# A four-layer graph network on one core: probability pieces at step ends in the score banks, own banks for second queries and keys, and a new order at several places

## The chip, the cores and the metric

The kernel runs on one core of one Trainium2 chip. The metric is the device time of one execution in microseconds (us), as the median of several runs. The engines are TensorE (PE: matmuls and transposes, whose weight loads are listed as PEld), VectorE (DVE), ScalarE (ACT), GpSimd (POOL) and SyncE (SP, which issues the DMAs here). Each has its own queue and works through it in order; they meet at semaphores.

## What is computed

`x` is 16 x 512 x 256, `adj` is a 512 x 512 matrix of zeros and ones. Four layers follow each other, each with a residual sum and a layer norm:

```python
x = _layernorm(x + L0(x, adj, Wq, Wk, Wv))   # rel = (x Wq^T)(x Wk^T)^T * adj^T, rows divided by their norm, times x Wv^T
x = _layernorm(x + L1(x, adj, weight, bias)) # normalized adjacency times x W, plus bias
x = _layernorm(x + L2(x, adj, adj, ...))     # three gated steps, below
x = _layernorm(x + L3(x, adj, ...))          # attention, 8 heads of 32, masked by adj, and an output product
```

One step of layer 2, done three times on h:

```python
a_in = a_out = einsum('nm,bmd->bnd', adj, h); av = concatenate([a_in, a_out])
z = sigmoid(lin(av, w3) + lin(h, u3));  r = sigmoid(lin(av, w4) + lin(h, u3))
hv = tanh(lin(av, w5) + lin(r * h, u5))
h = (1 - z) * h + z * hv
```

## The kernel before, in words

**Passes.** `passes` (L196) runs the body of every engine 18 times. In pass k, batch i = k goes through layers 0 to 2, batch t = k - 1 through the third norm and attention, and batch o = k - 2 through the rest of its attention (pieces 14 and 15, the last values product, the output product) and the fourth norm. Where a role has no batch (at the start and the end) its parts are left out. The order of the work in every queue is written out by hand, one role's instructions between the other's.

**High and low words.** A product with fp32 accuracy is made of three matmuls (`mm3`, L842 to L845): high by high, low by high, high by low. So every operand is split: ACT copies the high words (the lines with `copy(..[H]..)`), DVE subtracts them from the source for the low words (`tile_lo`, L659, and others). TensorE waits for both.

**PSUM** has eight banks, `ps[:, 0]` to `ps[:, 7]`. Banks 0 to 3 serve layers 0 to 2, banks 4 and 5 the two score tiles of a pair, the x3 transposes and the output product, bank 6 (PT_BANK) the transposed probabilities, bank 7 (O_BANK) the values product. The first queries and keys, `qk_of(0)` and `qk_of(1)`, use banks 6 and 7, the second ones, `qk_of(2)` and `qk_of(3)`, banks 0 and 1 (`QK_BANK`, L120).

**Layers 0 to 2 of batch i.** `y_of` (x times a product of weights), `gram` (four tiles, L967, the relation), DVE's mask product `rel_of` (L678), the relation product into u, the square sums (L1036 to L1042: POOL adds squares, sixteen small matmuls sum them, DVE copies them at L730, POOL takes the power -0.5 at L326), the sums and statistics of the first norm (L653, L627, L634, L639; POOL's power at L293), `gather` (L862, the adjacency product) of layer 1, its weight product, the second norm (`normalize`, L644), the transposes of the state (L1084), and then three steps j of layer 2: u3, gather, w4, w5, wd, u5 on TensorE; gate tanh L503 and L514 and value tanh L527 on ACT; the chain L819, L821, L822 on DVE, once for each half d, that makes the new state; the transposes of the state L1167 back to natural order, and its low words L826 and L829.

**Attention of batch t.** It has 32 score tiles in 16 pairs k. `score(k)` (L921) writes the two tiles of a pair to banks 4 and 5; DVE's `masked` (L672) masks them and finds the row maximum; ACT's `exponentials` (L395); POOL's `probabilities` inverts the row sum (L298) and scales (L304); TensorE's `back(k, c)` transposes the pair in two pieces c of four 128 x 128 blocks each (L945) into bank 6; ACT's `prob_copy` (L390) empties the bank; after four pairs a `values` product (L957). Step j of layer 2 has the pairs Z, D_, A, B_, C, E = 4j + 2 to 4j + 7 between its products. Piece (k, c) waits for the copy of the piece before it, since all use bank 6:

```python
            pe.wait_ge(pt_c, b * TILES + (2 * k + c))
```

The end of a step on TensorE, before:

```python
            if t is not None:
                back(t, A, 0)
                values(t, j)
                back(t, A, 1)
                if j == 0:
                    score(E)
            ...
            for d in range(DT):
                ...   # wait for h_f, four transposes of the state half d, L1167
                if t is not None:
                    back(t, B_, d)
```

**Queues beside it.** SP issues four small DMAs for each of the eight head slots (L238). Those of heads 4 to 7 wait for the score tiles of pairs 4 to 7 (L234). POOL splits the input x (L286, L288) right behind the powers of the third norm, and subtracts the low words of the next x^T (L268) late in the pass.

Of the kernel before, what the change touches and what calls it, by code (L numbers as in the profile page):

```python
# [19 lines left out]
def gnn_stack(nc, x, x_t, adj, wq0, wk0, wv0, w1, b1, w3, bw3, u3, bu3, w4, bw4, w5, bw5, u5, bu5,  # L20
# [16 lines left out]
    with ExitStack() as ctx:  # L37
# [82 lines left out]
        QK_BANK = (6, 7, 0, 1)  # L120
# [8 lines left out]
        def half(c):  # L129
            return slice(2 * c, 2 * c + 2)  # L130

# [228 lines left out]
        def _(act):  # L360
# [22 lines left out]
            def body(i, t, o):  # L383
                def prob_copy(b, k, c):
# [5 lines left out]
                    copy(pT[:, k % SLOTS, half(c)], ps[:, PT_BANK, :].rearrange("p (a b) -> p a b", a=2)).then_inc(pt_c, 1)  # L390
# [92 lines left out]
                for j in range(STEPS):  # L483
# [27 lines left out]
                    if i is not None:  # L511
                        for d in range(DT):
                            act.wait_ge(z_ps, m + (d + 1))
                            nc.scalar.activation(tz[:, d], ps[:, 2 + d], ACT.Tanh, bias=cols[:, BZ, d:d + 1],  # L514
                                                 scale=0.5).then_inc(z_t, 1)
                        if j == STEPS - 1:
                            xT_hi(i + 1)
                    if t is not None:
                        if j == 0:
                            exponentials(t, A)  # L520
                        prob_copy(t, D_, 0)
# [9 lines left out]
                    if i is not None and j < STEPS - 1:  # L531
                        h_hi(0)
                    if t is not None:
# [3 lines left out]
                    if i is not None and j < STEPS - 1:  # L537
                        h_hi(1)
                    if t is not None:
                        prob_copy(t, B_, 0)  # L540
# [4 lines left out]
                    if t is not None:  # L545
                        prob_copy(t, B_, 1)
# [4 lines left out]
        def _(dve):  # L551
# [58 lines left out]
            def body(i, t, o):  # L610
# [94 lines left out]
                if i is not None:  # L705
                    rel_of(0)
# [5 lines left out]
                if i is not None:  # L712
                    rel_lo(0)
                    rel_of(1)
# [10 lines left out]
                if t is not None:  # L725
                    qk_lo(0)
                    qk_lo(1)
                if i is not None:
                    dve.wait_ge(ssq_ps, i + 1)
                    nc.vector.tensor_copy(ssq[:, :], ps[:, 0, 0:NT]).then_inc(ssq_c, 1)  # L730
                    dve.wait_ge(rn_r, i + 1)
# [28 lines left out]
                if t is not None:  # L760
                    qk_lo(2)
                    qk_lo(3)
                if i is not None:
                    normalize(xg, xg, 1, 0, i, x2_r)
                    normalize(xg, xg, 1, 1, i, x2_r)
                    for c in range(2):
                        dve.wait_ge(xn_h, i * 6 + (c + 1))
                        TT(XNS[:, L, half(c)], xg[:, half(c)], f32(XNS[:, H, half(c)]), ALU.subtract).then_inc(xn_l, 1)
                if t is not None:
                    masked(1)  # L770
                if i is not None:
# [67 lines left out]
        def _(pe):  # L839
# [22 lines left out]
            def gather(xs, ready, value, signal):  # L862
# [9 lines left out]
                pe.wait_ge(ready, value + 1)  # L872
                node_tile(1, 0, (H,))
# [44 lines left out]
            def body(i, t, o):  # L918
                first = isinstance(i, int) and i == 0

                def score(k):  # L921
# [5 lines left out]
                    for u in range(2):  # L927
                        if k > 0:
                            pe.wait_ge(ttr, t * TILES + (2 * k - 1 + u))
                        q = 2 * (k % 8 // 4) + u  # L930
# [3 lines left out]
                def back(b, k, c):  # L934
                    if c == 0:
                        pe.wait_ge(nrm, b * TILES + (2 * k + 2))
                    if k == 0 and c == 0:
                        pe.wait_ge(vv_r, b + 1)
                    else:
                        pe.wait_ge(pt_c, b * TILES + (2 * k + c))  # L940
                    dst = ps[:, PT_BANK, :].rearrange("p (a b) -> p a b", a=2)
# [7 lines left out]
                def values(b, m):  # L949
                    gr, hf = m // 2, m % 2  # L950
                    pe.wait_ge(pt_c, b * TILES + 8 * (m + 1))
                    if m == 2:
# [14 lines left out]
                def gram(s):  # L967
                    c = slice(s * P, (s + 1) * P)
                    for d in range(DT):
# [17 lines left out]
                if i is not None:  # L987
                    if not first:
                        pe.wait_ge(x3a, i * 2)
                    gram(0)  # L990
                if o is not None:
                    back(o, 15, 0)
                if i is not None:
                    gram(1).then_inc(s_ps, 1)
# [102 lines left out]
                for j in range(STEPS):  # L1097
                    Z, D_, A, B_, C, E = [4 * j + k for k in range(2, 8)]
                    if i is not None:
# [55 lines left out]
                    if t is not None:  # L1155
# [3 lines left out]
                        if j == 0:  # L1159
                            score(E)  # L1160
# [38 lines left out]
```

## Time and profile before

| | us |
|---|---|
| runs | 2326.36, 2326.69, 2326.75 |
| median | 2326.69 |
| the profiled execution, its own time | 2327.76 |
| its span, first to last instruction | 2326.0 |
| TensorE busy in the span | 2099.9 (90%) |
| DVE busy | 1548.3 (67%) |
| ACT busy | 1267.0 (54%) |
| POOL busy | 979.5 (42%) |

The page of the profile gives shares of the span; since the kernel repeats one pass, a stretch of the timeline from one `y_of` to the next is the better thing to read. Pass 8 runs from 1112.4 to 1249.5 us. In a timeline a row is a start, a duration, the engine and line, what is written and read, how often, and, in brackets, how long the engine idled before it and which instruction ended that. Matmuls overlap, so their durations add up to more than their starts show.

### The profile page before, as it was taken

The page shows a single profiled execution, that of the slowest core. Times are in us where ns is not written, and L with a number is a line of the kernel's source. Part 1 is how long each engine was busy: PE and PEld are TensorE (multiplying, and loading weights), DVE is VectorE, ACT ScalarE, POOL GpSimd, SP SyncE. Part 2 cuts the span into 40 slices and gives each one's busy share as a digit, 9 for nine tenths or more (in the row PEclk, how much of TensorE's full clock was granted, in tenths as well). Part 3 has the DMA queues.
Part 4 walks back from the last instruction along what each step waited for, and adds up shares of the span by engine and source line. Part 5 has one row for each costly group of instructions (what it writes and reads, how often), then busy time and mean ns, then how long its engine had stood idle before and what let it go on. Part 6 is the DMA issues. An engine that isn't in the chain of part 4 may idle for free.

```text
span 2326.0 us, 34745 instructions
## 1 busy us (share of the span) xinstructions
PE 2099.9 (90%) x12342; PEld 1655.9 (71%) x12342; DVE 1548.3 (67%) x3423; ACT 1267.0 (54%) x2516; POOL 979.5 (42%) x1138
## 2 busy tenths in 40 slices
PE   5888999999999999999999999999999999999965
PEld 4666777777777777777777777777777777777743
DVE  5556676676667667666776767677676767767642
ACT  3235646566564656646465564646556464655644
POOL 3013534445353444535444453444435344443533
PEclk8899999999999999999999999999999999999987
DMA  3003021120202112021120301112030111202030
GB/s 122 1 19 70 7 52 46 37 64 19 63 20 55 46 37 64 19 53 30 52 50 28 73 19 41 42 39 62 19 73 28 37 46 37 64 19 67 16 90 10
DMA packets 65617, 101.16 MB, mean 43 GB/s; under 512 B 11425, under 2 KB 31137, under 8 KB 65441
## 3 DMA queue, kind: packets, MB, share of 16 engines
q1 hardware_dynamic: 65440, 98.87, 16.7%
q8 instruction: 103, 1.69, 0.3%
q14 instruction: 74, 0.60, 0.1%
HBM read 23.34 MB, written 8.39 MB: 14 GB/s over the span
## 4 chain that ended last, share of the span: by engine, by line
PE 62%; DVE 21%; ACT 9%; issue 6%; POOL 2%; DMA 1%; SPq 0%; DVEq 0%; POOLq 0%; ACTq 0%
PE ps L843 12%; PE ps L845 12%; PE ps L844 12%; PE ps L865 11%; PE ps L945 6%; PE ps L931 4%; DVE fa L821 4%; DVE fa L819 3%; DVE stats L627 3%; ACT pT L390 2%; DVE xn L653 2%; ACT fa L395 2%; DVE xn L644 2%; PE ps L957 2%; DVE fa L822 2%
## 5 line engine op out<-in xcount | busy, mean ns | idle before, releaser
L672 DVE CUSTOM_DVE_ANT_0 fa<-ps,mask 128x512 f32<-128x512 f32 x512 | 332.1, 685 | 284.8 <-PE ps L931 284.5
L298 POOL TENSOR_TENSOR rsum<-esum,mhalf 128x2 f32<-128x2 f32 x256 | 199.1, 778 | 756.4 <-ACT fa L395 756.4
L304 POOL TENSOR_SCALAR fa<-fa,rsum 128x512 f32<-128x512 f32 x512 | 421.7, 837 | 53.0 <-POOL rsum L298 53.0
L945 PE MATMUL ps<-ident,fa 128*128 128x128 f32 x2048 | 325.3, 282 | 97.7 <-ACT pT L390 85.7
L390 ACT COPY pT<-ps 128x512 f32<-128x512 f32 x512 | 298.8, 584 | 172.6 <-PE ps L945 172.6
L945 PEld LDWEIGHTS ps<-ident,fa 128*128 128x128 f32 x2048 | 243.6, 143 | 205.3 <-ACT pT L390 89.9
L395 ACT ACTIVATE fa<-fa,nmax 128x512 f32<-128x512 f32 x512 | 366.0, 724 | 32.2 <-DVE nmax L672 32.2
L659 DVE TENSOR_TENSOR ra<-ps,ra 128x512 fp32r<-128x512 f32 x224 | 151.1, 686 | 244.2 <-ACT ra L493 140.6
L865 PE MATMUL ps<-adjT,ra 128*128 128x512 f32 x1024 | 259.6, 407 | 27.5 <-DVE ra L745 25.3
L865 PEld LDWEIGHTS ps<-adjT,ra 128*128 128x128 f32 x1024 | 195.8, 194 | 79.0 <-issue 33.5
L931 PE MATMUL ps<-ra 128*128 128x512 f32 x512 | 179.8, 433 | 4.8 <-DMA ra<-ra 4.7
L293 POOL TENSOR_TENSOR rstd<-veps,mhalf 128x2 f32<-128x2 f32 x128 | 96.7, 762 | 168.1 <-DVE veps L639 168.1
L843 PE MATMUL ps<-ra,W_u 128*128 128x512 f32 x384 | 158.7, 413 | 0.0
L843 PE MATMUL ps<-ra,W_w 128*128 128x512 f32 x384 | 155.0, 404 | 0.0
L844 PE MATMUL ps<-ra,W_u 128*128 128x512 f32 x384 | 153.2, 399 | 0.0
L845 PE MATMUL ps<-ra,W_u 128*128 128x512 f32 x384 | 153.0, 398 | 0.0
L845 PE MATMUL ps<-ra,W_w 128*128 128x512 f32 x384 | 152.2, 396 | 0.0
L844 PE MATMUL ps<-ra,W_w 128*128 128x512 f32 x384 | 152.0, 396 | 0.0
L514 ACT ACTIVATE fa<-ps,cols 128x512 f32<-128x512 f32 x96 | 66.3, 690 | 114.0 <-PE ps L845 114.0
L957 PE MATMUL ps<-pT,vf 128*32 128x256 f32 x2048 | 127.7, 391 | 0.7 <-ACT pT L390 0.7
L493 ACT CAST ra<-ps 128x512 fp32r<-128x512 f32 x96 | 56.3, 586 | 115.0 <-PE ps L865 115.0
L843 PE MATMUL ps<-ra 128*128 128x512 f32 x256 | 107.6, 420 | 8.1 <-DVE ra L659 6.0
(183 smaller groups left out, 4653.1 us busy)
## 6 DMA issues: line engine op xcount, KB each, us to landing
ra<-ra SPq DMA_DIRECT2D x512, 128.0 KB, 2.4
fa<-in_x_T SPq DMA_DIRECT2D x17, 512.0 KB, 4.7
fa<-in_x SPq DMA_DIRECT2D x17, 512.0 KB, 3.9
out<-fa SPq DMA_DIRECT2D x16, 512.0 KB, 2.9
fa<-in_L_gnn_w_w SPq DMA_DIRECT2D x3, 512.0 KB, 8.3
adj_n<-in_adj SPq DMA_DIRECT2D x1, 1024.0 KB, 5.6
fa<-in_L_gnn_u_w SPq DMA_DIRECT2D x2, 256.0 KB, 9.3
fa<-in_L_gnn_Wk SPq DMA_DIRECT2D x1, 256.0 KB, 5.8
```

The lines of the kernel that those rows point to most:

```text
L298: nc.gpsimd.tensor_tensor(rsum[:, 2 * k:2 * k + 2], esum[:, 2 * k:2 * k + 2], mhalf[:, 4:6], ALU.pow).then_inc(rs_r, 1)
L304: nc.gpsimd.tensor_scalar(SC[:, g], SC[:, g], rsum[:, 2 * k + u:2 * k + u + 1], 1.0, ALU.mult, ALU.mult).then_inc(nrm, 1)
L390: copy(pT[:, k % SLOTS, half(c)], ps[:, PT_BANK, :].rearrange("p (a b) -> p a b", a=2)).then_inc(pt_c, 1)
L395: nc.scalar.activation(SC[:, s % RING], SC[:, s % RING], ACT.Exp, bias=nmax[:, s:s + 1], scale=-1.0, accum_out=esum[:, s:s + 1]).then_inc( ...
L672: nc.vector.tensor_tensor_reduce(out=SC[:, s % RING], in0=ps[:, 4 + u], in1=mask[:, 2 * (k % 8 // 4) + u], scale=-1.0, scalar=3.0e38, op0= ...
L843: mm(dst, w_h, m_h, start=first, stop=False, skip_group_check=again)
L844: mm(dst, w_l, m_h, start=False, stop=False, skip_group_check=again)
L845: return mm(dst, w_h, m_l, start=False, stop=last, skip_group_check=again)
L865: ins = mm(ps[:, q, :], xs[:, p, s, q * P:(q + 1) * P], adjT[:, H, s], start=s == 0 and p == H, stop=s == NT - 1 and p == L)
L931: mm(ps[:, 4 + u, :], STK[:, slot, 0, q * P:(q + 1) * P], STK[:, slot, 1, :], start=True, stop=True).then_inc(sc_ps, 1)
L945: ins = nc.tensor.transpose(dst[:, a, u * P:(u + 1) * P], SC[:, (2 * k + u) % RING, kt * P:(kt + 1) * P], ident[:, :])
L957: ins = mm(ps[e * HD:(e + 1) * HD, O_BANK, hf * 2 * P:(hf + 1) * 2 * P], vf[:, kt, head * HD:(head + 1) * HD], pT[:, (4 * m + e) % SLOTS, kt],
```

## The change

1. `pt_bank(k, c)`: the pieces of pairs 5, 9 and 13 (B_ of each step) go to banks 4 and 5 instead of bank 6. They wait for the masking of the score tiles that are in these banks, not for the copy of the piece before; score pairs 7 and 12 wait for their copies.
2. TensorE at the end of a step: piece (B_, d) comes ahead of the transposes of the state half d, not behind. `score(7)` moves from the end of step 0 to step 1, between u3 and the gather.
3. ACT: in step 0 the copy of piece (D_, 0) and the exponentials of A move between the two tanh of the z gate. At the end of every step the copies of the pieces of A come ahead of the high copy of the first state half, and both pieces of B_ ahead of the high copies of the transposed state.
4. Second queries and keys go to banks 1 and 7 instead of 0 and 1. `qk_of(3)` waits for the copy of the values' input (vv_r), the gather of step 0 waits for the low words of the second queries only behind its first two node tiles, the first values product for all four.
5. DVE: the second norm's `normalize` comes ahead of `qk_lo(2)` and `qk_lo(3)`, of which one moves between the two low-word subtractions of the normed state and one behind `masked(1)`.
6. DVE: the copy of the square sums comes ahead of `qk_lo(1)`.
7. DVE: the third norm's `normalize` comes ahead of the mask product `rel_of(0)`.
8. TensorE: piece (15, 0) of the old batch moves between the two halves of `gram(0)`.

```diff
-        QK_BANK = (6, 7, 0, 1)
+        QK_BANK = (6, 7, 1, 7)
+        def pt_bank(k, c):
+            return 4 + c if k in (5, 9, 13) else PT_BANK
...
-                    if i is not None:
-                        for d in range(DT):
+                    for d in range(DT):
+                        if i is not None:
                             act.wait_ge(z_ps, m + (d + 1))
                             nc.scalar.activation(tz[:, d], ps[:, 2 + d], ACT.Tanh, bias=cols[:, BZ, d:d + 1],
                                                  scale=0.5).then_inc(z_t, 1)
-                        if j == STEPS - 1:
-                            xT_hi(i + 1)
+                        if t is not None and j == 0 and d == 0:
+                            prob_copy(t, D_, 0)
+                            exponentials(t, A)
+                    if i is not None and j == STEPS - 1:
+                        xT_hi(i + 1)
                     if t is not None:
-                        if j == 0:
-                            exponentials(t, A)
-                        prob_copy(t, D_, 0)
+                        if j > 0:
+                            prob_copy(t, D_, 0)
...
                         prob_copy(t, A, 0)
-                    if i is not None and j < STEPS - 1:
-                        h_hi(0)
-                    if t is not None:
                         prob_copy(t, A, 1)
                         if j == STEPS - 1:
                             exponentials(t, E)
                     if i is not None and j < STEPS - 1:
+                        h_hi(0)
+                    if t is not None:
+                        prob_copy(t, B_, 0)
+                    if i is not None and j < STEPS - 1:
                         h_hi(1)
                     if t is not None:
-                        prob_copy(t, B_, 0)
+                        prob_copy(t, B_, 1)
...
-                if i is not None:
-                    rel_of(0)
                 if t is not None:
...
                     normalize(x3, xg, 2, 0, t)
                     normalize(x3, xg, 2, 1, t, x3_r)
                 if i is not None:
+                    rel_of(0)
                     rel_lo(0)
...
                     qk_lo(0)
-                    qk_lo(1)
                 if i is not None:
                     dve.wait_ge(ssq_ps, i + 1)
                     nc.vector.tensor_copy(ssq[:, :], ps[:, 0, 0:NT]).then_inc(ssq_c, 1)
+                if t is not None:
+                    qk_lo(1)
...
-                if t is not None:
-                    qk_lo(2)
-                    qk_lo(3)
                 if i is not None:
                     normalize(xg, xg, 1, 0, i, x2_r)
                     normalize(xg, xg, 1, 1, i, x2_r)
-                    for c in range(2):
+                for c in range(2):
+                    if i is not None:
                         dve.wait_ge(xn_h, i * 6 + (c + 1))
                         TT(XNS[:, L, half(c)], xg[:, half(c)], f32(XNS[:, H, half(c)]), ALU.subtract).then_inc(xn_l, 1)
+                    if t is not None and c == 0:
+                        qk_lo(2)
                 if t is not None:
                     masked(1)
+                    qk_lo(3)
...
                 node_tile(0, 1)
                 pe.wait_ge(ready, value + 1)
+                if second is not None:
+                    pe.wait_ge(second, second_value)
...
+                        if k in (7, 12):
+                            pe.wait_ge(pt_c, t * TILES + (2 * (5 if k == 7 else 9) + u + 1))
...
+                    elif pt_bank(k, c) == PT_BANK:
+                        pe.wait_ge(pt_c, b * TILES + (2 * k + c - (2 if c == 0 and pt_bank(k - 1, 1) != PT_BANK else 0)))
                     else:
-                        pe.wait_ge(pt_c, b * TILES + (2 * k + c))
+                        pe.wait_ge(ttr, b * TILES + (2 * (k + (1 if k == 5 else 2)) + c + 1))
...
+                    if m == 0:
+                        pe.wait_ge(qk_l, b * 4 + 4)
...
-                    gram(0)
+                    gram(0, (0,))
                 if o is not None:
                     back(o, 15, 0)
                 if i is not None:
+                    gram(0, (1,))
                     gram(1).then_inc(s_ps, 1)
...
                     qk_of(2)
+                    pe.wait_ge(vv_r, t + 1)
                     qk_of(3)
...
-                        elif t is not None:
-                            pe.wait_ge(qk_l, t * 4 + 4)
-                        gather(XNS, xn_l, m + 1, a_ps)
+                    if t is not None and j == 1:
+                        score(7)
+                    if i is not None:
+                        gather(XNS, xn_l, m + 1, a_ps, qk_l if j == 0 and t is not None else None, (t or 0) * 4 + 3)
...
-                        if j == 0:
-                            score(E)
...
                     for d in range(DT):
+                        if t is not None:
+                            back(t, B_, d)
                         if i is not None:
                             pe.wait_ge(h_f, m + (d + 1))
...
-                        if t is not None:
-                            back(t, B_, d)
```

## Rows read from the trace of the kernel before

**Rows 1.** The page's first line: span and instructions.
```profile
span 2326.0 us, 34745 instructions
```

**Rows 2.** Windows: stretch, its length, busy us (instructions) by engine, clock, DMA share, GB/s.
```profile
1112.40:1249.50 137.10, 128.21 (x772) 101.75 (x771) 95.66 (x214) 78.28 (x156) 60.95 (x71) 1.00 0.17 43
...
2209.00:2300.00 91.00, 60.87 (x366) 40.68 (x364) 35.35 (x103) 46.52 (x105) 37.73 (x56) 0.79 0.24 58
```

**Rows 3.** Waits of TensorE in pass 8: us in total, times, longest.
```profile
PE ps L945 <- ACT pT L390: 4.3, 7, 1.2
```

**Rows 4.** Timeline of TensorE around the ends of steps 2, 0 and 1.
```profile
1112.05 0.66 PE L945 MATMUL ps<-ident,fa 128*128 128x128 f32 x4
1112.46 0.48 PE L843 MATMUL ps<-ra,W_g 128*128 128x512 f32 x1
...
1182.17 0.40 PE L845 MATMUL ps<-ra,W_u 128*128 128x512 f32 x1
1183.82 0.66 PE L945 MATMUL ps<-ident,fa 128*128 128x128 f32 x4 [1.25 <-ACT pT L390]
...
1191.39 0.66 PE L1167 MATMUL ps<-ident,fa 128*128 128x128 f32 x4 [0.19 <-DVE fa L822]
...
1192.94 0.48 PE L843 MATMUL ps<-ra,W_u 128*128 128x512 f32 x1
...
1219.66 0.66 PE L1167 MATMUL ps<-ident,fa 128*128 128x128 f32 x4 [0.20 <-DVE fa L822]
...
1221.20 0.48 PE L843 MATMUL ps<-ra,W_u 128*128 128x512 f32 x1
```

**Rows 5.** Timeline of TensorE in the first half of pass 8.
```profile
1117.40 0.50 PE L843 MATMUL ps<-ra 128*128 128x512 f32 x1 [0.34 <-DVE ra L659]
...
1123.87 1.09 PE L1004 MATMUL ps<-ident,xn 128*128 128x128 f32 x8 [0.47 <-DVE xn L644]
...
1126.76 0.50 PE L843 MATMUL ps<-ra 128*128 128x512 f32 x1
...
1146.84 3.98 PE L865 MATMUL ps<-adjT,ra 128*128 128x512 f32 x16 [1.08 <-DVE ra L745]
...
1161.67 3.97 PE L865 MATMUL ps<-adjT,ra 128*128 128x512 f32 x16 [0.17 <-DVE ra L768]
```

**Rows 6.** Timeline of DVE in pass 8.
```profile
1120.24 1.23 DVE L678 TENSOR_TENSOR fa<-ps,adj_n 128x1024 f32<-128x1024 f32 x1 [2.40 <-PE ps L845]
1121.38 2.44 DVE L644 TENSOR_SCALAR xn<-xn,mv,rstd 128x256 f32<-128x256 f32 x4
...
1137.89 0.75 DVE L686 SCALAR_TENSOR_TENSOR ra<-ps,cols,ra 128x512 fp32r<-128x512 f32 x1 [2.44 <-ACT ra L419]
1138.55 0.15 DVE L730 COPY ssq<-ps 128x4 f32<-128x4 f32 x1
1139.84 0.88 DVE L653 SCALAR_TENSOR_TENSOR xn<-ps,rnorm,fa 128x256 f32<-128x256 f32 x2 [1.14 <-POOL rnorm L326]
...
1159.42 1.37 DVE L644 TENSOR_SCALAR xn<-xn,mv,rstd 128x256 f32<-128x256 f32 x4
...
1186.40 0.69 DVE L819 TENSOR_TENSOR fa<-fa 128x512 f32<-128x512 f32 x1 [0.19 <-ACT fa L527]
...
1219.52 1.46 DVE L826 TENSOR_TENSOR ra<-fa,ra 128x512 fp32r<-128x512 f32 x2
```

**Rows 7.** Timeline of ACT in pass 8.
```profile
1160.18 1.26 ACT L473 CAST ra<-xn 128x512 fp32r<-128x512 f32 x2 [0.17 <-DVE xn L644]
...
1181.20 0.69 ACT L514 ACTIVATE fa<-ps,cols 128x512 f32<-128x512 f32 x1 [1.62 <-PE ps L845]
...
1183.19 0.57 ACT L390 COPY pT<-ps 128x512 f32<-128x512 f32 x1
```

**Rows 8.** Timeline of POOL in pass 8.
```profile
1120.29 2.41 POOL L288 TENSOR_TENSOR ra<-fa,ra 128x1024 fp32r<-128x1024 f32 x1
...
1186.54 2.21 POOL L304 TENSOR_SCALAR fa<-fa,rsum 128x512 f32<-128x512 f32 x2 [0.21 <-POOL rsum L298]
```

More of the change, by code:

```diff
@@ L389, in prob_copy @@
                     act.wait_ge(pt_ps, b * TILES + (2 * k + c + 1))
-                    copy(pT[:, k % SLOTS, half(c)], ps[:, PT_BANK, :].rearrange("p (a b) -> p a b", a=2)).then_inc(pt_c, 1)
+                    copy(pT[:, k % SLOTS, half(c)], ps[:, pt_bank(k, c), :].rearrange("p (a b) -> p a b", a=2)).then_inc(pt_c, 1)
                 def exponentials(b, k):
@@ L544, in body @@
                             copy(XNS[:, H, half(c)], natural(0)[:, half(c)]).then_inc(xn_h, 1)
-                    if t is not None:
-                        prob_copy(t, B_, 1)
             passes(body)
@@ L860, in natural_tiles, with gather @@
                 return ins
-            def gather(xs, ready, value, signal):
+            def gather(xs, ready, value, signal, second=None, second_value=0):
                 def node_tile(q, s, parts=(H, L)):
@@ L938, in back @@
                         pe.wait_ge(vv_r, b + 1)
-                    else:
-                        pe.wait_ge(pt_c, b * TILES + (2 * k + c))
-                    dst = ps[:, PT_BANK, :].rearrange("p (a b) -> p a b", a=2)
+                    elif pt_bank(k, c) == PT_BANK:
+                        pe.wait_ge(pt_c, b * TILES + (2 * k + c - (2 if c == 0 and pt_bank(k - 1, 1) != PT_BANK else 0)))
+                    else:
+                        pe.wait_ge(ttr, b * TILES + (2 * (k + (1 if k == 5 else 2)) + c + 1))
+                    dst = ps[:, pt_bank(k, c), :].rearrange("p (a b) -> p a b", a=2)
                     for a in range(2):
@@ L965, in y_of, with gram @@
                     ins.then_inc(y_ps, 1)
-                def gram(s):
+                def gram(s, ds=(0, 1)):
                     c = slice(s * P, (s + 1) * P)
-                    for d in range(DT):
+                    for d in ds:
                         if s == 0:
@@ L1102, in body @@
                             u3_of(j)
-                        elif t is not None:
-                            pe.wait_ge(qk_l, t * 4 + 4)
-                        gather(XNS, xn_l, m + 1, a_ps)
+                    if t is not None and j == 1:
+                        score(7)
+                    if i is not None:
+                        gather(XNS, xn_l, m + 1, a_ps, qk_l if j == 0 and t is not None else None, (t or 0) * 4 + 3)
                     if t is not None:
@@ L1170, in body @@
                                     ins.then_inc(tp_ps, 1)
-                        if t is not None:
-                            back(t, B_, d)
             passes(body)
```

## The prediction

> **What bounds the kernel now.** I read the span first, then one whole pass of the loop, then that pass engine by engine. The kernel is 18 passes over 16 batches, with the first three layers of batch i and attention of batch i-1 interleaved. A steady pass takes 137.1 us and the matmul unit works for 128.21 of them, at the full granted clock, DVE for 95.66 and ACT for 78.28 [rows 2]. So TensorE's queue, which runs in order, sets the period, and only its 8.9 us of waits can be won. Half of these, 4.3 us in seven waits, stand before transposes of probability pieces (L945) and are put down to ACT's copy of the piece before [rows 3]: all pieces go through one PSUM bank, so a piece cannot start until ACT has emptied it. The rest are a few tenths each, before transposes of the state at a step's end, before the third norm's transposes, and 1.08 us before the gather of layer 1 [rows 4, 5]. An engine that resumes after a wait also pays the drain of its last matmul: two transposes' blocks in a row start 0.41 us apart (1112.05 and 1112.46) while one followed by a wait is booked with 0.66 us [rows 4]. So removed waits return 0.1 to 0.2 us more than their label.
>
> **Part by part,** in the clock of pass 8.
>
> *Step ends, steps 1 and 2.* Pieces of pair B_ go to banks 4 and 5 and come ahead of the state transposes rather than behind. They then fill the time in which DVE still makes the state. What is late next is the state: the second transposes cannot start before 1219.66 in step 1, whatever the pieces do [rows 4]. Behind them stood one wait and a piece; u3 began at 1221.20. Now u3 follows the transposes directly, but needs the low words of the state, which DVE starts at 1219.52 and makes in two instructions, 1.46 us in all, the first done about 1220.15 [rows 4, 6]. u3 starts at 1220.25: **0.95 us** won, 0.6 if ACT's high copy is late, 1.1 at most. In step 2 the next thing is the product y of the next pass, which needs none of this: it moves up by the last piece, from 1112.46 to about 1111.95: **0.5 us** (0.4 to 0.6).
>
> *Step 0.* Three edits meet. ACT now copies piece (3,0) and does pair 4's exponentials before its second gate tanh. That tanh began at 1181.20 after 1.62 us of idleness, and only behind it and two exponentials came the copy, at 1183.19, so TensorE, done with u5's first half by 1182.41 (its last matmul starts at 1182.17, and such matmuls follow each other by 0.24), waited until 1183.82 [rows 4, 7]. In the new order the copy is done by 1180.0, the exponentials fill the idle time (two cost 1.4 us: the tanh is over at 1181.8, the copy starts at 1183.19), the tanh is 0.2 late, and TensorE goes on at 1182.4. All behind is 1.42 us earlier: the value tanh and the DVE chain behind it, which began at 1186.40 [rows 6], at 1184.95. Now POOL's scaling of pair 5 meets this chain's first instruction instead of its second (it took 2.21 us for two [rows 8]); I add 0.2. The second state transposes, 4.99 us after the chain's start, come at 1190.1 against 1191.39, and u3 at 1190.7 against 1192.94 [rows 4]. But score tile 7, which stood ahead of the transposes, is now between u3 and the gather and costs its 0.47 there. Net 2.25 less 0.47: **1.8 us** (1.2 if the chain lags, 2.3 if POOL keeps clear). Its cost elsewhere: masking and exponentials of pair 7 come later, in front of ACT's high copy of the gather's result. They need some 2.9 us from the tile's start; that copy is due 2.3 us after the gather's, 2.8 after the tile's. I count nothing, since the low words had a slack of 0.5 us before TensorE wants them. SP's head copies that wait for this tile are used ten microseconds later.
>
> *Start of the pass.* The first tile of the Gram product waits 0.34 us between its halves for DVE's low words of y [rows 5]. Piece (15,0) now stands in that gap; its own condition, the copy of the piece before, allows **0.3 us** (0 to 0.5). Next, the third norm. DVE did the mask product first (1120.24, 1.23 us), then four scalings in 2.44 us, then TensorE's transposes at 1123.87 after 0.47 us of waiting [rows 5, 6]. With the scalings ahead of the mask product they fall into DVE's idle time before 1120.24, and the transposes follow the Gram product at once: **0.6 us** (0 to 0.7). The mask product is late by up to a microsecond against its inputs; the relation product at 1126.76 stood behind transposes and values and has about that much room.
>
> *Square sums.* DVE copied them at 1138.55, only after the second keys' low words, though TensorE had made them before the keys' product, while DVE idled for 2.44 us before 1137.89; copied at 1135.7 instead, they are through POOL by 1137.0. POOL's power and DVE's sums, which waited 1.14 us, came at 1139.84 [rows 6]. With the copy first the sums wait only for DVE's low words and the first half of their product, both at 1138.65. The whole chain to the gather of layer 1 moves by 1.15, and TensorE has other work until 1145.6: **1.1 us** of the 1.08 plus drain (0.8 to 1.2).
>
> *Second queries and keys* in banks 1 and 7. The second norm's scalings no longer stand behind two low-word instructions (they began at 1159.42 [rows 6]); but ACT's high copy at 1160.18 stood behind a piece's copy and can come only 0.25 us earlier [rows 7]. The queries' low words, 0.66 us, now sit between the two halves that the gather needs, and the gather, started 0.25 earlier than 1161.67 [rows 5], waits inside for the second half. The two cancel: **0** (-0.4 to +0.8, the upper end if ACT's copies slip in earlier). The added waits for v_ready and qk_l at the values product were satisfied tens of microseconds before.
>
> *Sum.* 0.5 + 0.3 + 0.6 + 1.1 + 0 + 1.8 + 0.95 = 5.25 us a pass. Fourteen passes (2 to 15) have all three roles: 73.5. Pass 1 lacks the old batch's pieces: 4.4. In pass 16, attention alone (91 us of it are 2209 to 2300), TensorE works 60.87 of 91 us [rows 2] and every piece waits 0.7 to 0.8 us for a copy; three pairs lose two such waits each, against a later score tile 7: 4.5 with the boundary before it (-1 to 8). Together 82.4. The profiled execution took 2327.76 us, its span 2326.0 [rows 1]: 2245.4. The median of the runs is 1.07 below that execution: **2244 us**.
>
> **The rivals.** *The third norm is caught by POOL.* For it: the four scalings took 2.44 us at 1121.38 against 1.37 at 1159.42, and their first ended just behind POOL's 2.41 us subtraction, begun at 1120.29 [rows 6, 8]. Moved up, the second two follow POOL's last power, and POOL's input split starts in the same moment. If that subtraction goes first, the norm ends at 1122.9, the mask product at 1124.1, its high copy (1.26 at most [rows 7]) at 1125.3, and the piece copy queued behind it on ACT holds the values product: the relation product starts at 1127.9, 1.1 later than now, not 1.4 earlier. 2.5 x 14 = 35: 2279 us. Against it: the input split comes ahead of the subtraction, and in step 1 (L803 followed by L801, with L304 waiting) POOL did not get between two DVE instructions that had no wait between them. 14%.
> The Trainium skill ("SBUF — State Buffer", SBUF: two separate sides) says that a GpSimd instruction and a DVE one using the shared port pair exclude each other for the whole instruction, whoever starts first. By that rule alone the sum would be 2244 or 2279, as the split or the subtraction is met first; the trace agrees with the rule at 1121.38, where the first scaling ends 0.15 us behind POOL.
>
> *More than I count.* POOL leaves the state chains alone (two instructions a step at 1.06 instead of 0.69), and the second norm gives its 0.8: 2.9 us more a pass, 2200 us. Against it: POOL's work must lie somewhere, and each step now shows such a meeting. 10%.
>
> *Slower: the pieces hold the state.* A B_ piece now stands ahead of the first state transposes and waits for POOL's scaling of its pair; if that is late, the recurrence waits with it, the very chain that was safe. Place: step ends; price: the lateness, three times a pass; it decides from 1.75 us a step, where the 5.25 are eaten. At 3 us a step a pass loses 9 - 5.25 = 3.75, 56 over 15 passes: 2383 us. For it: in step 0 the scaling ends only 0.9 us before the piece is due. Against: in steps 1 and 2 it was done 5 us before. 4%.
>
> *The waits re-form, nothing won.* The state chain, not TensorE, could be what a step lasts; then pieces moved from behind to ahead change nothing but where TensorE idles, and other gains are absorbed by it: 2326 us. Against: between steps TensorE is unbroken for 20 us, and what comes earlier there stays earlier. 4%.
>
> **How the numbers follow.** Forecast 68%, own range 2226 to 2262 (the bounds above, taken together, give 1.2 us a pass either way). The lock rival lifts the upper end to 2284; 2200, 2326 and 2383 stay out, 18%. 0.2%, about 4.7 us, is what a measurement can tell. Faster: 68 + 14 + 10, 0.92; same 0.04; slower 0.04.
>
> **What would show it.** Period near 131.8 us with TensorE's busy time still near 128; L945's waits for ACT down from 4.3 to under 2 us a pass; no wait of 1.25 in step 0; about 1 us before the second state transposes in each step (new, larger than now); sums right behind the second keys' low words; the gather of layer 1 without its wait; four scalings before the mask product, ended by 1120.6 in this clock. I am wrong if transposes of x3 wait for DVE by over 1 us, if the gather in step 1 or the products after it wait on ACT's high copy, or if the first state transposes start behind POOL.

## The result and the profile after

The changed kernel takes 2264.02 us (2263.49 to 2266.11, four runs) against 2326.72 before: ratio 0.9732, 95% interval 0.9715 to 0.9749. It is faster by 62.7 us, not by the 82.4 that were summed. 2244 was forecast, the range of 2226 to 2284 holds the result, and the forecast's own range, to 2262, ends just below it.

Line numbers have moved: L649 is the norms' scaling (L644 before), L683 the mask product, L691 the queries' and keys' low words, L850 to L852 `mm3`, L872 the gather, L958 the pieces, L972 the values product, L1185 the transposes of the state. The page of the kernel after, first line and busy row of section 1:

```profile
span 2264.3 us, 34780 instructions
...
PE 2079.4 (92%) x12342; PEld 1658.8 (73%) x12342; DVE 1582.8 (70%) x3423; ACT 1259.3 (56%) x2516; POOL 972.9 (43%) x1138
```

Pass 8 after, as a window (length, busy us of PE, PEld, DVE, ACT, POOL, clock):

```profile
1086.49:1219.70 133.21, 126.81 (x772) 101.87 (x770) 97.70 (x213) 77.95 (x158) 60.45 (x71) 1.00 0.18 44
```

Against [rows 2] the pass is 3.9 us shorter. TensorE's 126.81 us are 1.4 less than before with the same 772 matmuls: presumably the drains of removed waits. DVE's 97.70 are 2.0 more with the same work; that is the first sign of what went wrong. TensorE's waits after, over 14 passes:

```profile
PE ps L1185 <- DVE fa L829: 34.7, 42, 0.9
PE ps L972 <- ACT pT L394: 22.4, 14, 1.6
PE ps L958 <- ACT pT L394: 16.6, 28, 0.8
PE ps L872 <- DVE ra L772: 11.2, 14, 1.1
```

The pieces wait 1.2 us a pass instead of 4.3 [rows 3]. The state transposes wait 0.8 in each step, where about 1 was forecast. The second row is new: the values product waits 1.60 us in every pass for the copy of its last piece. Before, it waited for nothing.

To see where each term lies I took the starts of the pass (y), of layer 1's gather (T) and of the three steps' gathers (a0, a1, a2), and the medians of their distances over passes 3 to 13 (numbered from 0). The period in the last column is the mean over the same passes, and so it is for every run below:

| us | y to T | T to a0 | a0 to a1 | a1 to a2 | a2 to y | mean period |
|---|---|---|---|---|---|---|
| before | 34.38 | 14.82 | 34.20 | 28.27 | 25.25 | 137.13 |
| after | 33.96 | 14.47 | 32.61 | 27.41 | 24.72 | 133.22 |
| forecast change | -2.0 | 0 | -1.8 | -0.95 | -0.5 | -5.25 |
| measured change | -0.42 | -0.35 | -1.59 | -0.86 | -0.53 | -3.91 |

The steps came as forecast. (The 0.35 won before a0 is not a gain of its own: the transposes of the second norm's result no longer wait, but the gather waits 0.8 us inside. So T to a1, -1.94, is what to hold against -1.8.) The five changes add up to 3.75 and not to 3.91, because in two of these passes of the kernel before, 7 and 13, the granted clock fell to 1.2 GHz for 3.4 us in step 0, which made each about 1.25 us longer; by medians the period is 136.91 before and 133.17 after, 3.74 less. More on this in the last section. All that is missing lies between y and T. The timeline of DVE after, the third norm and what follows:

```profile
1092.64 4.27 DVE L649 TENSOR_SCALAR xn<-xn,mv,rstd 128x256 f32<-128x256 f32 x4 [0.78 <-POOL rstd L297]
1096.84 1.21 DVE L683 TENSOR_TENSOR fa<-ps,adj_n 128x1024 f32<-128x1024 f32 x1
```

POOL in the same stretch:

```profile
1091.82 1.38 POOL L297 TENSOR_TENSOR rstd<-veps,mhalf 128x2 f32<-128x2 f32 x2 [3.38 <-DVE veps L644]
1093.19 1.10 POOL L290 TENSOR_SCALAR ra<-fa 128x1024 fp32r<-128x1024 f32 x1
1094.37 2.40 POOL L292 TENSOR_TENSOR ra<-fa,ra 128x1024 fp32r<-128x1024 f32 x1
```

ACT, and then TensorE:

```profile
1098.08 1.04 ACT L417 CAST ra<-fa 128x1024 fp32r<-128x1024 f32 x1 [5.55 <-DVE fa L683]
1099.03 0.58 ACT L394 COPY pT<-ps 128x512 f32<-128x512 f32 x1
```

```profile
1095.15 0.60 PE L958 MATMUL ps<-ident,fa 128*128 128x128 f32 x4
...
1096.98 1.08 PE L1020 MATMUL ps<-ident,xn 128*128 128x128 f32 x8
1099.66 1.93 PE L972 MATMUL ps<-pT,vf 128*32 128x256 f32 x32 [1.60 <-ACT pT L394]
1101.53 0.50 PE L850 MATMUL ps<-ra 128*128 128x512 f32 x1
```

The four scalings take 4.27 us, worse than the 2.44 in their old place and three times the 1.37 of the undisturbed ones [rows 6]. They end at 1096.91, 0.14 behind POOL's subtraction (1094.37 + 2.40). The mask product follows, then its high copy, and only then, in ACT's queue, the copy of piece (15, 1), whose transposes had ended at 1095.75, over three microseconds before ACT took it up. The relation product starts 15.04 us after y; before it was 14.30 (1126.76 - 1112.46 [rows 4, 5]). This is the forecast's lock rival.

### The profile page after: what moved, and what is told of

The parts are those of the page before. It is cut to its first block, busy times and chain, and to the rows that moved or that the text cites. A ratio compares the mean times of both kernels' runs of the same rounds, so it can differ in the third digit from the quotient of the medians.

```text
span 2264.3 us, 34780 instructions
## 1 busy us (share of the span) xinstructions
PE 2079.4 (92%) x12342; PEld 1658.8 (73%) x12342; DVE 1582.8 (70%) x3423; ACT 1259.3 (56%) x2516; POOL 972.9 (43%) x1138
## 3 DMA queue, kind: packets, MB, share of 16 engines
q1 hardware_dynamic: 65440, 98.87, 17.2%
## 4 chain that ended last, share of the span: by engine, by line
PE 70%; DVE 17%; ACT 7%; issue 4%; POOL 1%; DMA 1%; SPq 0%; DVEq 0%; POOLq 0%; ACTq 0%
PE ps L850 15%; PE ps L852 15%; PE ps L851 15%; PE ps L872 10%; PE ps L958 5%; PE ps L942 5%; DVE fa L828 4%; DVE fa L826 3%; DVE xn L649 3%; ACT pT L394 2%; PE ps L972 2%; DVE fa L829 2%; ACT fa L533 1%; PE ps L1185 1%; PE ps L1056 1%
## 5 line engine op out<-in xcount | busy, mean ns | idle before, releaser
L308 POOL TENSOR_SCALAR fa<-fa,rsum 128x512 f32<-128x512 f32 x512 | 411.5, 816 | 53.0 <-POOL rsum L302 53.0
L958 PE MATMUL ps<-ident,fa 128*128 128x128 f32 x2048 | 311.1, 279 | 40.1 <-ACT pT L394 31.3
L958 PEld LDWEIGHTS ps<-ident,fa 128*128 128x128 f32 x2048 | 246.1, 143 | 126.5 <-ACT pT L394 40.5
L872 PE MATMUL ps<-adjT,ra 128*128 128x512 f32 x1024 | 260.7, 404 | 21.6 <-DVE ra L772 11.9
L872 PEld LDWEIGHTS ps<-adjT,ra 128*128 128x128 f32 x1024 | 191.8, 191 | 77.5 <-DVE ra L772 22.9
L942 PE MATMUL ps<-ra 128*128 128x512 f32 x512 | 178.8, 430 | 6.3 <-DMA ra<-ra 4.7
L850 PE MATMUL ps<-ra,W_u 128*128 128x512 f32 x384 | 158.6, 413 | 1.1
L850 PE MATMUL ps<-ra,W_w 128*128 128x512 f32 x384 | 154.9, 403 | 0.0
L852 PE MATMUL ps<-ra,W_u 128*128 128x512 f32 x384 | 153.3, 399 | 0.0
L852 PE MATMUL ps<-ra,W_w 128*128 128x512 f32 x384 | 152.1, 396 | 0.0
L972 PE MATMUL ps<-pT,vf 128*32 128x256 f32 x2048 | 127.5, 391 | 23.1 <-ACT pT L394 23.1
L649 DVE TENSOR_SCALAR xn<-xn,mv,rstd 128x256 f32<-128x256 f32 x192 | 110.9, 633 | 16.6 <-POOL rstd L297 16.5
L972 PEld LDWEIGHTS ps<-pT,vf 128*32 128x32 f32 x2048 | 61.0, 112 | 70.2 <-ACT pT L394 26.8
```

The lines of the kernel that those rows point to most:

```text
L308: nc.gpsimd.tensor_scalar(SC[:, g], SC[:, g], rsum[:, 2 * k + u:2 * k + u + 1], 1.0, ALU.mult, ALU.mult).then_inc(nrm, 1)
L850: mm(dst, w_h, m_h, start=first, stop=False, skip_group_check=again)
L852: return mm(dst, w_h, m_l, start=False, stop=last, skip_group_check=again)
L872: ins = mm(ps[:, q, :], xs[:, p, s, q * P:(q + 1) * P], adjT[:, H, s], start=s == 0 and p == H, stop=s == NT - 1 and p == L)
L942: mm(ps[:, 4 + u, :], STK[:, slot, 0, q * P:(q + 1) * P], STK[:, slot, 1, :], start=True, stop=True).then_inc(sc_ps, 1)
L958: ins = nc.tensor.transpose(dst[:, a, u * P:(u + 1) * P], SC[:, (2 * k + u) % RING, kt * P:(kt + 1) * P], ident[:, :])
```

## The experiments

Eleven kernels, each made from the changed one. The theory: POOL's input split and DVE's scalings exclude each other, and this reaches TensorE through the mask product and ACT's queue. The rival: the norm's new place is worth its 0.6 us, and the missing time lies elsewhere.

**norm_back** undoes one part:

```diff
                     variance("t", 2, 1, n1)
+                if i is not None:
+                    rel_of(0)
...
                     normalize(x3, xg, 2, 1, t, x3_r)
                 if i is not None:
-                    rel_of(0)
                     rel_lo(0)
```

> The changed kernel with one part undone: DVE's mask product rel_of(0) again ahead of the third norm's scalings. Theory (POOL's subtraction of the input split gets between the last two scalings, and the mask product, its high copy on ACT and piece (15, 1) behind it are late, so the values product waits 1.60 us a pass): this part of the change is a loss; undone, the 1.60 us before the values product go, about 0.5 us come back before the x3 transposes, and the time falls from 2264 by about 1.0 us in each of 14 passes, to 2250. Rival (the values product waits for its piece whatever DVE does, because ACT takes it after the high copy, and the norm's new place gives the predicted 0.6 us): the time rises to about 2272.

2252.62 us, ratio to before 0.9681 (0.9664 to 0.9697), period 132.47. The part is a loss of 0.75 us a pass (1.0 was expected). The wait of the values product is gone, that of the x3 transposes is back with 0.8 us:

```profile
PE ps L1021 <- DVE xn L649: 11.0, 14, 0.8
```

**pool_waits** leaves DVE's new order and takes away what it meets:

```diff
                     rstd_of(2, t)
                 if i is not None:
+                    if t is not None:
+                        gp.wait_ge(x3_r, t + 1)
                     split_x(i)
```

> The changed kernel, with POOL's split of the input x held back until the third norm is done (one added wait of POOL on x3_r). Theory: DVE's four scalings then take 1.4 us instead of 4.3 from the first's start to the last's end, the mask product starts 2.5 us earlier or as soon as the Gram tiles allow, the values product does not wait; the relation product starts 1.6 us earlier in each of 14 passes: 2264 falls to 2241. The split ends about 0.6 us later than now, with 2 us of room. Rival (the port has no part in it): the scalings stay slow, the values product waits as before, 2264 or a little above.

2241.04 us, ratio 0.9627 (0.961 to 0.9643), period 131.47. DVE's and POOL's timelines:

```profile
1078.17 1.38 DVE L651 TENSOR_SCALAR xn<-xn,mv,rstd 128x256 f32<-128x256 f32 x4 [0.78 <-POOL rstd L297]
1079.47 1.22 DVE L685 TENSOR_TENSOR fa<-ps,adj_n 128x1024 f32<-128x1024 f32 x1
1081.81 2.59 DVE L689 TENSOR_TENSOR ra<-fa,ra 128x1024 fp32r<-128x1024 f32 x1 [1.11 <-ACT ra L419]
```

```profile
1079.78 1.06 POOL L290 TENSOR_SCALAR ra<-fa 128x1024 fp32r<-128x1024 f32 x1 [1.06 <-DVE xn L651]
1080.92 2.40 POOL L292 TENSOR_TENSOR ra<-fa,ra 128x1024 fp32r<-128x1024 f32 x1
```

The same four scalings take 1.38 us. POOL's subtraction now meets the low words of the relation (2.59 us instead of 1.23), which have room: the values product starts at 1083.43 behind the x3 transposes without a wait. POOL has room too: its subtraction ends at 1083.32, and the relation product, which by the code needs it, starts at 1085.29. With this one wait added, the part is worth 1.75 us a pass more than without, and 1.0 more than the old order.

**act_first** breaks the chain at its other end:

```diff
+                if o is not None:
+                    prob_copy(o, 15, 1)
                 if i is not None:
                     rel_hi(0)
-                if o is not None:
-                    prob_copy(o, 15, 1)
```

> The changed kernel, with ACT's copy of piece (15, 1) ahead of the high copy rel_hi(0). Theory (the wait of the values product comes through ACT's queue): DVE's scalings stay at 4.3 us with POOL between them, but the values product does not wait; what is late next is DVE's first low words of the relation, so the relation product starts about 0.9 us earlier, not 1.6: 2264 falls to 2251. Rival (the wait comes from the copy of piece (15, 1) itself or from the transposes of x3): no change, 2264.

2259.72 us, ratio 0.9711 (0.9695 to 0.9727), period 132.90. The values product no longer waits, so the wait did come through ACT's queue, but only 0.3 us a pass is won, not 0.9. What is late next is DVE's low words of the relation, twice a pass, 1.0 us in all (14 passes):

```profile
PE ps L850 <- DVE ra L687: 13.9, 28, 0.6
```

I had counted the wait for the first pair of tiles and not that for the second, which the delay of the whole DVE queue also reaches.

**ssq_back** puts the copy of the square sums behind `qk_lo(1)` again.

> The changed kernel with the copy of the square sums again behind the second keys' low words. Expected by the step of the prediction (1.1 us a pass from this part): the wait before layer 1's gather comes back with about 1.1 us, 15 passes: 2264 rises to 2280. Rival (the relation's delay covers it, nothing was won here): 2264.

2286.93 us, period 134.40: 1.18 us a pass, all of it between y and T (35.12 against 33.96). The wait before the gather is back:

```profile
PE ps L870 <- DVE ra L749: 15.7, 14, 1.4
```

The total rose by 22.9 where 15 passes make 17.7; about 4 of the rest are in the last two passes, on which more below.

**tanh_back** restores ACT's order in step 0 (both tanh, pair 4's exponentials, piece (3, 0)).

> The changed kernel with ACT's order in step 0 undone: both gate tanh, then pair 4's exponentials, then the copy of piece (3, 0). By the step of the prediction: TensorE waits for that copy again, 1.25 us and its drain, and everything behind it in the step is later by 1.4 us, 15 passes: 2264 rises to 2285, and the wait before L958 of about 1.25 us is back. Rival (the wait before the second state transposes, 0.79 us a step, already covers it): the time rises by half of that or less, 2272 or under.

2283.28 us, period 134.76: 1.54 us a pass, all of it in step 0 (a0 to a1 34.17 against 32.61). The total rose by 19.3 and not by the 23 of 15 passes, since the last two passes took 4 us less. The wait stands where it stood before the change:

```profile
1166.68 0.66 PE L958 MATMUL ps<-ident,fa 128*128 128x128 f32 x4 [1.25 <-ACT pT L394]
```

**bank_back** makes `pt_bank` return bank 6 for every piece; their place ahead of the state transposes stays.

> The changed kernel with all pieces in bank 6 again, in their new order ahead of the state transposes. If the banks carry the gain at step ends: pieces (B_, 0) and (B_, 1) wait for copies again, and the second, in front of the second state transposes, holds them by about 0.35 us in each of three steps; 15 passes: 2264 rises to 2280. Rival (the order alone did it, since TensorE waits 0.8 us for the second state half anyway and the copies fit into that): 2264 to 2268.

2292.59 us, ratio 0.986 (0.9845 to 0.9875), period 134.41: 1.19 us a pass. It isn't spread as expected (0.35 a step) but 0.14, 0.13 and 0.96 in steps 0, 1 and 2. The end of step 2:

```profile
1225.66 0.63 PE L958 MATMUL ps<-ident,fa 128*128 128x128 f32 x4 [0.82 <-POOL fa L308]
1226.13 0.60 PE L1185 MATMUL ps<-ident,fa 128*128 128x128 f32 x4
1227.46 0.66 PE L958 MATMUL ps<-ident,fa 128*128 128x128 f32 x4 [0.73 <-ACT pT L394]
```

Both pieces wait, and the product y cannot start before them, since it has no wait of its own to hide them in; in steps 0 and 1 the wait for the state covers most of it. (POOL is named for the first, but the instruction it ended then scales pair 14. By the code piece (13, 0) waits for the copy of (12, 1).) So in step 1 the order alone gives 0.73 of the 0.86 us, and at step 2 it is a loss: a2 to y is 25.68 us here, 25.25 in the kernel before. The rival is nearly right in steps 0 and 1 and wrong in step 2.

**x2_back** puts `qk_lo(2)` and `qk_lo(3)` ahead of the second norm's scalings again, in the new banks.

> The changed kernel with DVE's order at the second norm undone: both low words of the second queries and keys ahead of its scalings; the banks 1 and 7 stay. By the prediction this part is worth nothing: 2264, within 4 us. Rival (it is worth what its place promises, the scalings begin 1.3 us earlier): 2264 rises by 0.5 us or more a pass, 2272 and up.

2267.15 us, ratio 0.9744 (0.9729 to 0.9759), period 133.11 against 133.22: worth nothing in a pass; undone, the period is even 0.1 us shorter. The total is 3 us higher because the last two passes took 115.6 us instead of 112.3. What banks 1 and 7 are worth by themselves was not tried; with DVE's old order on top of them T to a0 is 14.74, against 14.82 before.

**best** is pool_waits, and on ACT the high copy of the first half ahead of piece (0, 1):

```diff
                     prob_copy(t, 0, 0)
-                    prob_copy(t, 0, 1)
-                if i is not None:
-                    for c in range(2):
+                for c in range(2):
+                    if i is not None:
                         act.wait_ge(x2_r, i * 2 + (c + 1))
                         copy(XNS[:, H, half(c)], xg[:, half(c)]).then_inc(xn_h, 1)
+                    if t is not None and c == 0:
+                        prob_copy(t, 0, 1)
```

> The kernel with POOL's wait for the third norm (2241), and with ACT's high copy of the first half of the normed state ahead of its copy of piece (0, 1). In the trace the scalings of that half end at 1116.19 while ACT idles until 1116.80 and does the piece first; the gather of step 0 starts at 1118.68 behind this chain and waits inside for the second half. Expected: the high copy 0.9 us earlier, the first low words as soon as DVE has done the norm, the second 0.7 earlier; the gather ends 0.7 us earlier in each of 15 passes: 2241 falls to 2231. Rival (the copy of piece (0, 1), now half a microsecond later, holds TensorE): 2241.

2223.87 us, ratio 0.9564 (0.9551 to 0.9577), period 130.62: 0.85 us a pass below pool_waits, all between T and a0 (13.65 against 14.49). So the second norm's part was blocked by one copy in ACT's queue, and gives what its place promised once the copy steps back. The total fell by 17.2 where 15 passes make 12.8. The swap on ACT was not tried with DVE's old order, but the trace of x2_back speaks to it: there the high copy waits for the scalings, so it could not have come earlier by a swap:

```profile
1132.12 1.27 ACT L477 CAST ra<-xn 128x512 fp32r<-128x512 f32 x2 [0.15 <-DVE xn L649]
```

So by that row the gain takes both edits.

**gram_back** puts piece (15, 0) behind the whole first Gram tile again.

> The changed kernel with piece (15, 0) again behind the whole first tile of the Gram product. By the prediction's step it gives 0.3 us a pass, 14 passes: 2264 rises to 2268. But in the changed kernel the end of the third norm (1096.92) and not the Gram product decides when the x3 transposes start, so the theory of POOL's hold says: nothing, 2264, and the 0.3 us wait before the Gram tile's second half comes back with a shorter wait elsewhere.

2265.1 us, ratio 0.9732 (0.9717 to 0.9747), period 133.19: nothing. Two rows of its waits show where it went:

```profile
PE ps L972 <- ACT pT L394: 19.1, 14, 1.4
...
PE ps L850 <- DVE ra L664: 4.7, 14, 0.3
```

The 0.3 us wait is back and the values product waits 0.24 less. In the changed kernel this part is hidden behind the third norm.

**score7_back** puts score tile 7 back at the end of step 0, with pair 5's pieces in bank 6.

> The changed kernel with score tile 7 back at the end of step 0, ahead of the pieces of pair 5, which therefore go to bank 6 again; the rest stays. If the price of the tile's move is its own 0.47 us between u3 and the gather, it is saved there; at the step's end the tile fills 0.5 us of the 0.79 us wait before the second state transposes, but the piece (5, 1) then waits for the copy of (5, 0) and holds those transposes by 0.3 us. Net 0.1 to 0.3 us a pass less: 2264 falls to 2261, at most unchanged. Rival (the move is what makes the step end work): 2270 and up.

2260.76 us, ratio 0.9715 (0.97 to 0.973), period 132.88: 0.34 us a pass less. This run undoes two things, the tile's move and the own banks of pair 5. Together they are a loss in step 0: the banks are worth less than the tile's move costs.

**best2** is best with ACT's high copy of the next x^T behind the copy of piece (11, 0).

> The kernel of the run best (2224) with ACT's high copy of the next x^T behind the copy of piece (11, 0) instead of ahead of it. TensorE waits 0.37 us for that piece's copy in step 2; that wait and its drain go, the low words on POOL and DVE have room: 0.45 us in each of 15 passes, 2224 falls to 2217. Rival (the copy of 1.04 us now delays pair 14's exponentials and with them a piece later): 2224.

2224.14 us, ratio 0.9556 (0.9543 to 0.9569): no change against best; the period is 130.50 against 130.62, so 0.12 us a pass is won where 0.45 was expected. TensorE's waits for pieces fell and those for the state rose. best2 first, then best:

```profile
PE ps L1189 <- DVE fa L833: 38.1, 42, 1.0
PE ps L962 <- ACT pT L396: 11.5, 14, 0.8
```

```profile
PE ps L1189 <- DVE fa L833: 34.8, 42, 0.9
PE ps L962 <- ACT pT L396: 16.6, 28, 0.8
```

Piece (11, 1) no longer waits, but ACT does the same work ahead of the value tanh, in another order. Most of the time won moves to the wait for the state chain, which begins with that tanh.

## Why the prediction was right or wrong

- **What bounds.** Right. TensorE's waits were what there was to win, and in most stretches a removed wait came back as time, drain included; the Gram tile's did not.
- **Step ends 1 and 2.** Right: 0.86 and 0.53 against 0.95 and 0.5, with the new wait of 0.8 to 0.9 us before the second state transposes. Of this the own banks carry 0.13 in step 1 (bank_back), and all of it in step 2, where the order alone costs 0.43. The prediction gave step 2 its 0.5 without saying that it hangs on the banks.
- **Step 0.** Right: 1.94 up to the gather of step 1 against 1.8. The tanh order carries 1.54 (1.42 was worked out). Score tile 7's move costs 0.34 net of what pair 5's own banks bring; if these bring the 0.14 of bank_back, the move itself costs about 0.48, as counted (0.47). POOL's scaling did meet the chain's first instruction.
- **Square sums.** Right in mechanism and size: 1.18 against 1.1.
- **Second norm.** Right: 0 as summed (x2_back 0.1 the other way), and for the reason given: ACT's copy, and a wait inside the gather. The upper bound of 0.8 was reached when the copy stepped back: 0.85.
- **Third norm.** Wrong, and this is the step that failed: "0.6 us (0 to 0.7)". Measured by undoing it, it costs 0.75, so the term was off by 1.35. Together with the Gram tile's 0.3, which came to nothing, that is what is missing between y and T (1.58), less what the square sums gave above their term. The room that the prediction gave the mask product, "up to a microsecond against its inputs", was overrun: it started 10.35 us after y, where it had started 7.78 after y before. The term's bounds left out a loss, although the rival beside it gave one: "that subtraction goes first, the norm ends at 1122.9", "the piece copy queued behind it on ACT holds the values product". It happened a little otherwise: the split (L290) held the third scaling, and the subtraction then got in before the fourth. The argument against the rival, that POOL did not get between two DVE instructions without a wait between them, is refuted by exactly this pair. The rival had the chain nearly right: norm's end 10.44 us after y (1122.9 - 1112.46), measured 10.42; relation product 15.44, measured 15.04. Its price of 2.5 a pass was too high first of all because it kept that chain at its old times, although y itself comes 0.5 earlier.
- **What held the scalings.** They take 4.27 us with POOL beside and 1.38 with POOL held back. The third ends 0.15 us behind POOL's split and the fourth 0.15 behind its subtraction, which itself takes 2.40 us whichever DVE instruction is beside it. The Trainium skill ("SBUF — State Buffer", SBUF: two separate sides) has a DVE and a GpSimd instruction that use the shared port pair exclude each other for the whole instruction. The runs agree with it: one side is held until about the other's end, and the other loses nothing.
- **Gram tile.** 0.3 forecast, nothing measured: its wait is gone and the time comes back in the next one, since the third norm ends later than the Gram product. So it is with the norm in its old place too: in norm_back y to T is 1.19 below the kernel before, which the square sums' 1.18 fill alone. Only with POOL held back do the two terms appear: y to T is 32.18 in pool_waits, 2.2 below before, so they give 1.0 together where 0.9 was summed.
- **The sum.** With the third norm freed the period falls by 5.66 (137.13 - 131.47; 5.5 by medians) and the time to 2241.04, where the forecast had 5.25 and 2244. That it fits so well is partly luck, since more was won in the passes and less behind them. Passes 16 and 17 (span after the start of pass 15, less one period) took 116.9 us before and 112.3 after, 4.7 less where 4.5 were summed. That isn't evidence for the 4.5: six kernels with the same instructions in these passes, after among them, take 110.7 to 116.2 us there (last section), and pool_waits with its 116.2 has almost none of this gain.

## What to carry to other kernels

When an instruction is moved into idle time, look at the other engines in that window, not only at its own queue: a DVE step of 1.4 us took 4.3 because two long instructions of POOL (1.10 and 2.40 us) began in the same moment, and one wait on POOL, which had two microseconds of room, was worth 1.75 us a pass. When a wait is taken away, ask which instruction is next in each queue that passes the result on: twice here (piece (15, 1) and piece (0, 1)) ACT did a copy in the wrong order, and once the swap was worth 0.85 us. And a wait removed beside a recurrence chain can come back in front of that chain's result, as in best2, unless the chain itself starts earlier.

## What was not expected of the hardware

**POOL got between two scalings that DVE issues one behind the other.** The third took 1.14 us, the fourth 2.56, while POOL's split and subtraction ran; the longest scaling of the x norms, after and with POOL held back (xcount, min/median/max ns):

```profile
L649 DVE TENSOR_SCALAR xn<-xn,mv,rstd x168: 404/410/2560, 293.0 to 2065.4; 128x256 f32<-128x256 f32 x168
```

```profile
L651 DVE TENSOR_SCALAR xn<-xn,mv,rstd x168: 403/409/416, 289.0 to 2037.0; 128x256 f32<-128x256 f32 x168
```

The third scaling had itself been waiting for POOL; in the case that I had reasoned from, the first DVE instruction had not. Whether that decides who is next wasn't tried.

**The last two passes differ by the clock.** The kernels after, norm_back, pool_waits, act_first, ssq_back and gram_back have the same instructions there, and take 110.7 to 116.2 us (worked out as above). Three of them as windows (the last fields: clock, DMA share, GB/s), act_first, after and ssq_back:

```profile
2146.60:2257.35 110.75, 70.61 (x443) 46.82 (x441) 40.94 (x119) 49.33 (x111) 41.72 (x61) 0.80 0.21 53
```

```profile
2152.05:2264.31 112.26, 71.97 (x444) 48.46 (x442) 40.85 (x119) 49.32 (x112) 41.84 (x61) 0.77 0.21 52
```

```profile
2168.65:2284.88 116.23, 76.35 (x443) 50.90 (x441) 40.94 (x119) 49.40 (x112) 41.88 (x61) 0.74 0.20 50
```

TensorE is busy for about 65% of this stretch, with waits of up to 2.5 us between, where in a steady pass it is busy for 95%. The granted clock changes between its two levels, 2.4 and 1.2 GHz, and the stretch is the longer the lower its mean: 0.80, 0.77, 0.74 of full speed here; the other three lie between or level (norm_back 113.6 us at 0.77, gram_back 113.7 at 0.76, pool_waits 116.2 at 0.74). The stretch is entered at other times in each kernel; whether that decides the clock stays open.

**The clock fell in two steady passes of the kernel before.** In pass 7 TensorE had just waited twice, 0.82 us for a piece's copy and 0.87 us for the second norm, when the granted clock fell to 1.2 GHz in the gather of step 0 and stayed there for 3.4 us; in the same place of pass 13 it did so again.

```profile
1020.48 0.65 PE L945 MATMUL ps<-ident,fa 128*128 128x128 f32 x4 [0.82 <-ACT pT L390]
1022.00 1.60 PE L1084 MATMUL ps<-ident,xn 128*128 128x128 f32 x8 [0.87 <-DVE xn L644]
```

The window with the low clock:

```profile
1022.86:1026.28 3.42, 3.42 (x11) 2.60 (x10) 3.42 (x8) 3.24 (x8) 0.00 (x0) 0.50 0.74 173
```

Each cost about 1.25 us. The passes beside them have the same waits and kept the full clock; why these two did not stays open. In none of the twelve other traces did the clock fall in passes 3 to 14. So about 0.2 us of the period's 3.91 come from the clock of the kernel before, which no term of the sum counts.

In totals that differ by a few microseconds the period of the steady passes is therefore the safer measure, and its median safer than its mean: bank_back's total rose by 28.6 us, of which 1.19 x 15 = 17.9 are in the passes and about 10 in the last two, where its pieces wait more as well.
